# A graph network kernel: one tile of gathered rows in 25, 64 and 32 fetched row by row from SP and ScalarE, and features and output as 112 and 15 partitions

## The reference

```python
x = _layernorm(x + _L0_gnn_ref(x, edge_attr_64, edge_index, ...))   # sums of edge_attr_64 by src and by dst, then an MLP
x = _layernorm(x + _L1_gnn_ref(x, edge_attr_16, u, ...))            # mean of edge_attr_16 by dst, then an MLP
x = _layernorm(x + _L2_gnn_ref(x, weight, src, dst, edge_type_16))  # x[src] @ weight[type], summed by dst
x = _layernorm(x + _L3_gnn_ref(x, edge_index, edge_attr_32, ...))   # MLP on x[src], x[dst], edge; mean and max by dst; MLP
```

## Time and profile before

| | |
|---|---|
| median of 3 runs | 13071.3 us |
| the three runs | 13071.3, 13152.06, 13070.82 us |
| the profiled execution's own time | 13160.62 us, span 13158.9 us |
| busy share POOL, DVE, PE, ACT | 73%, 47%, 21%, 10% |
| mean granted clock of TensorE | 0.558 |
| first edge stage | about 280 to 4250 us |
| second edge stage | 4798 to 8718 us |
| third edge stage | 9035 to 12917 us |
| last node stage | 12928 to 13159 us |

### The profile page before, as it was taken

How to read it: one execution, slowest core, us unless ns; L and a number is a source line. 1 busy time by engine, 2 the same in 40 slices (tenths; PEclk the granted TensorE clock), 3 DMA queues, 4 the chain that set the end, 5 groups by cost and what they waited for, 6 DMA issues and landing times. The chain is left out here.

```text
span 13158.9 us, 78994 instructions
## 1 busy us (share of the span) xinstructions
PE 2819.3 (21%) x12129; PEld 1989.0 (15%) x12156; DVE 6175.8 (47%) x21573; ACT 1273.1 (10%) x3641; POOL 9662.0 (73%) x10101
## 2 busy tenths in 40 slices
PE   2000011111100740000000000013444444444446
PEld 2000011111100420000000000012232332332233
DVE  8877357777733432222222222224555555555554
ACT  3111011111110320000000000000000000001011
POOL 7777757777777747777777777777777777777774
PEclk6555555555555665555555555555666666666665
DMA  5444334444443332222222222222222222222221
GB/s 168 119 118 115 108 106 118 117 116 118 115 119 108 124 103 66 65 66 64 67 64 67 64 67 64 67 51 55 66 66 66 66 64 66 65 66 66 66 66 32
DMA packets 731549, 1103.24 MB, mean 84 GB/s; under 512 B 240731, under 2 KB 347192, under 8 KB 730567
## 3 DMA queue, kind: packets, MB, share of 16 engines
q0 software_dynamic: 332944, 306.83, 12.6%
q1 hardware_dynamic: 231478, 567.25, 11.4%
q10 hardware_dynamic: 167040, 228.30, 5.7%
HBM read 548.64 MB, written 552.93 MB: 84 GB/s over the span
## 5 line engine op out<-in xcount | busy, mean ns | idle before, releaser
L130 POOL DMA_INDIRECT msg<-Y,idx x3125 | 2965.9, 949 | 1060.1 <-issue 951.8
L130 POOL DMA_INDIRECT g<-in_edge_attr,idxs x3072 | 2948.7, 960 | 1017.7 <-issue 858.3
L130 POOL DMA_INDIRECT yg<-ytab,idx x3125 | 2951.8, 945 | 962.4 <-issue 950.0
L1520 DVE SCALAR_TENSOR_TENSOR run<-run,same,msg 128x64 f32<-128x64 f32 x3125 | 890.7, 285 | 3030.5 <-DMA msg<-Y,idx 2923.0
L584 DVE SCALAR_TENSOR_TENSOR run<-run,sameD 128x80 f32<-128x80 f32 x3072 | 906.3, 295 | 1396.9 <-DMA g<-in_edge_attr,idxs 875.2
L1914 DVE SCALAR_TENSOR_TENSOR run<-run,same,ps 128x32 f32<-128x32 f32 x3125 | 774.9, 248 | 1640.7 <-PE ps L1808 1538.0
L1108 PE MATMUL ps<-tail,before 128*128 128x64 f32 (+2 forms) x10 | 2.8, 422 | 4575.7 <-PEq L1422 3931.0
L1897 DVE SCALAR_TENSOR_TENSOR zx<-zx,same,zs 128x32 f32<-128x32 f32 x3124 | 792.1, 254 | 136.7 <-DVE anew L1880 29.1
L588 DVE SCALAR_TENSOR_TENSOR runS<-runS,sameS,g 128x64 f32<-128x64 f32 x3072 | 850.3, 277 | 0.0
L1789 PE MATMUL ps<-eaT,W1e 128*128 128x512 f32 (+1 forms) x394 | 401.6, 1123 | 1962.7 <-DMA yg<-ytab,idx 1962.1
L952 PE MATMUL ps<-hot 128*98 128x128 bf16 x3072 | 373.1, 315 | 1891.0 <-DVE hot L680 1891.0
(11 more groups left out here) (339 smaller groups left out, 6217.2 us busy)
## 6 DMA issues: line engine op xcount, KB each, us to landing
R<-run SPq DMA_DIRECT2D x390, 320.0 KB, 2.3
R<-run SPq DMA_DIRECT2D x195, 512.0 KB, 2.7
R<-run SPq DMA_DIRECT2D x124, 800.0 KB, 3.8
v<-in_edge_attr ACTq DMA_DIRECT2D x384, 256.0 KB
RA<-runS SPq DMA_DIRECT2D x256, 256.0 KB, 3.0
Y<-tab SPq DMA_DIRECT2D x98, 512.0 KB, 2.7
msg<-Y,idx POOLq DMA_INDIRECT x3125, 2.4
Z<-zeros SPq DMA_DIRECT2D x125, 400.0 KB, 4.3
```

The costliest lines, as they stand in the source:

```text
L130: eng.indirect_dma_start(out=out, out_offset=None, in_=table, in_offset=bass.IndirectOffsetOnAxis(ap=index, axis=0)).then_inc(sem, 16)
L1520: ins_ = v.scalar_tensor_tensor(out=run[:, q, t, :], in0=prev, scalar=same[:, q, t:t + 1], in1=msg[:, q, t, :], op0=ALU.mult, op1=ALU.add)
```

## The change

- In `edges_2` tile 12 of each slot's 25 is no longer gathered by POOL. Slots 0, 2 and 4 of a chunk leave it to SP, slots 1 and 3 to ACT: the engine loads 32 row offsets from a list into registers, issues 32 DMAs of one row each, and does that four times (`row_tile`, `fetch_rows`). Then it asks for the next chunk's list (`list_rows`). DVE waits for those rows by `by_row`.
- In `edges_3` the same for tile 8 of slot 1 of each of the 48 chunks, all by SP.
- In `edges_01` tile 7 of slot 3 in all chunks but 0 and CHB: partitions 0 to 63 by SP, 64 to 127 by ACT, in pieces of 24, 20 and 20 rows behind three of the four slots (`row_pieces`).
- The lists of byte offsets are computed by DVE (`list_tiles`, and two instructions in `chores`) and put to memory with partitions and columns exchanged: 128x32 and 128x64 elements for the first stage, 128x130 and 128x49 for the others. The last two puts stand on SP behind the load of x.
- x is loaded and the output stored as 112 + 15 partitions in place of 127; the one partition that is left (12,500 = 127 x 98 + 54) is as before.
- `nodes_3` keeps the 896 columns of a group as four stacks of 32 rows in 128 partitions by 256 columns. W4 is placed by zero columns around it (`W4z`), W5 is a block diagonal (`W5e`), W6 stands once per stack (`W6e`). The relus work on 128x256 in place of 32x512 and 32x384.

```diff
+MOSTP = LASTP // 16 * 16
+STACK = P // 32
...
+ROW_AT2, ROW_AT3, ROW_SLOT3 = 12, 8, 1
+ROW_REGS = 32
+ROW_Q1, ROW_AT1 = NQ - 1, SG - 1
+PIECES1 = ((0, 24), (24, 20), (44, 20))
+SP_ROWS = (0, 2, 4)
...
+def fetch_rows(nc, eng, offsets, out, table, size, sem):
+    n = out.shape[0]
+    for a in range(0, n, ROW_REGS):
+        _, rows = nc.values_load_multi_w_load_instructions(
+            offsets[0:1, a:min(a + ROW_REGS, n)], engines=[eng.engine], min_val=0, max_val=table.shape[1] - size,
+            skip_runtime_bounds_check_because="the byte at which a row of the table begins")
+        for i, row in enumerate(rows):
+            eng.dma_start(out[a + i:a + i + 1, :].bitcast(U8), table[:, bass.ds(row, size)]).then_inc(sem, 16)
 
...
+        def list_rows(eng, i, c):
+            eng.dma_start(lists1[:, i, :], k.rows1[bass.ds(c, 1), i * P // 2:(i + 1) * P // 2]).then_inc(listed[i], 16)
+        def row_piece(eng, i, c, j):
+            a, n = PIECES1[j]
+            if j == 0:
+                eng.wait_ge(listed[i], 16)
+                eng.sem_clear(listed[i])
+            fetch_rows(nc, eng, lists1[:, i, a:a + n], g64[i * P // 2 + a:i * P // 2 + a + n, ROW_Q1, ROW_AT1, :], e64_bytes,
+                       4 * D, by_row)
+            if j == len(PIECES1) - 1:
+                if isinstance(c, int) and c == CHB - 1:
+                    eng.wait_ge(rows1_put, 32)
+                    list_rows(eng, i, CHB + 1)
+                elif not (isinstance(c, int) and c == C2 - 1):
+                    list_rows(eng, i, c + 1)
+        def row_pieces(eng, i, c, q):
+            if q == NQ - 1:
+                if not (isinstance(c, int) and c + 1 in (CHB, C2)):
+                    row_piece(eng, i, c + 1, 0)
+            elif q < len(PIECES1) - 1 and by_rows(c):
+                row_piece(eng, i, c, q + 1)
 
...
+                if q == ROW_Q1 and by_rows(c):
+                    v.wait_ge(by_row, 16 * P)
+                    v.sem_clear(by_row)
                 v.wait_ge(metas, n + 1)
-                v.wait_ge(got[q], 16 * SG * (c + 1))
+                if q == ROW_Q1:
+                    v.wait_ge(got[q], 16 * gathered(c))
+                else:
+                    v.wait_ge(got[q], 16 * SG * (c + 1))
...
+            def chunk(c, out, c0):
                 for q in range(NQ):
-                    turn_over(c, q, RB, 0)
+                    turn_over(c, q, out, c0)
+                    row_pieces(sp, 0, c, q)
...
+            chunk(CHB - 1, RB, 0)
             sp.wait_ge(x_clear, 1)
-            sp.dma_start(k.X[0:LASTP, :, :], ins["x"][0:LASTP * NB, :].rearrange("(p b) f -> p b f", b=NB)).then_inc(settled, 16)
+            for a, z in ((0, MOSTP), (MOSTP, LASTP)):
+                sp.dma_start(k.X[a:z, :, :], ins["x"][a * NB:z * NB, :].rearrange("(p b) f -> p b f", b=NB)).then_inc(settled, 16)
             sp.dma_start(k.X[LASTP:LASTP + 1, 0:LASTN, :],
...
-                    turn_over(c, q, RA, CHB)
+            sp.wait_ge(rows_listed, 2)
+            for to, rows in ((k.rows2, rows2[:, :, :].rearrange("p c q -> p (c q)")), (k.rows3, rows3[:, :])):
+                sp.dma_start(to.rearrange("n p -> p n"), rows, allow_slow_non_contiguous=True).then_inc(settled, 16)
+            chunk(CHB, RA, CHB)
+            with sp.Fori(CHB + 1, CE) as c:
...
-                    for t in range(SG):
+                    for t in range(SG - (q == ROW_Q1 and by_rows(c))):
                         gather(pool, g64[:, q, t, :], ins["edge_attr_64"], idxs[:, q, t:t + 1], got[q])
...
                     iteration(c, q, idxA if last else idxB, sameA if late else sameB, CHB if last else 0, CHB if late else 0)
+                    row_pieces(act, 1, c, q)
...
+        def row_tile(eng, c, q):
+            eng.wait_ge(listed[q], 16)
+            eng.sem_clear(listed[q])
+            fetch_rows(nc, eng, lists[:, q, :], msg[:, q, ROW_AT2, :], Yb, 4 * D, by_row[q])
...
+            for q in SP_ROWS:
+                row_tile(sp, 0, q)
             with sp.Fori(0, LAST) as c:
                 for q in range(NS2):
                     slot(c, q)
+                    if q in SP_ROWS:
+                        row_tile(sp, c + 1, q)
             for q in range(NS2 - 1):
                 slot(LAST, q)
...
+                        row_tile(act, c, q)
+            for q in range(NS2):
...
                 for t in range(SL2):
+                    if t == ROW_AT2:
+                        continue
                     gather(pool, msg[:, q, t, :], k.Y, idx[:, q, t:t + 1],
                            late[t // PART2] if last_slot(c, q) else got[q])
 
...
                         if last_slot(c, q):
-                            v.wait_ge(late[t // part], 16 * part)
+                            v.wait_ge(late[t // part], 16 * (part - (t // part == ROW_AT2 // part)))
+                            if t // part == ROW_AT2 // part:
+                                v.wait_ge(by_row[q], 16 * P * CHUNKS2)
                         else:
-                            v.wait_ge(got[q], 16 * SL2 * (c + 1))
+                            v.wait_ge(got[q], 16 * (SL2 - 1) * (c + 1))
+                            v.wait_ge(by_row[q], 16 * P * (c + 1))
...
+            def row_tile(c):
+                sp.wait_ge(listed, 16)
+                sp.sem_clear(listed)
+                fetch_rows(nc, sp, lists[:, :], yg[:, ROW_SLOT3, ROW_AT3 * MSG:(ROW_AT3 + 1) * MSG], ytab, 4 * MSG, by_row)
+                list_rows(c + 1)
+            list_rows(0)
+            row_tile(0)
+            with sp.Fori(0, LAST) as c:
                 for q in range(NS3):
                     store(c, q)
+                    if q == ROW_SLOT3:
+                        row_tile(c + 1)
+            for q in range(NS3):
+                store(LAST, q)
+            sp.wait_ge(listed, 16)
...
                 for a, b, w in cuts(steps):
                     nc.tensor.matmul(ps(1, q)[0:w, a:b], k.W1e[0:w, 0:w], eaT[0:w, m, a:b], start=True, stop=False)
+                    if a == 0:
+                        if by_rows(c, q):
+                            pe.wait_ge(by_row, 16 * P)
+                            pe.sem_clear(by_row)
+                        pe.wait_ge(got[q], 16 * (SL3 - (q == ROW_SLOT3)) * c + 16 * (steps - by_rows(c, q)))
...
                 a, z = g0 * GB, g1 * GB
-                sp.dma_start(most[:, a:z, :], k.X[0:LASTP, a:z, :]).then_inc(saved, 16)
-                saves += 1
+                for i, j in ((0, MOSTP), (MOSTP, LASTP)):
+                    sp.dma_start(most[i:j, a:z, :], k.X[i:j, a:z, :]).then_inc(saved, 16)
+                    saves += 1
...
-                last.then_inc(outp, 1)
+                both = psY[q][:, 0:(GB - 1) * D].rearrange("p (j c f) -> p j c f", c=2, f=D)
+                nc.tensor.matmul(both[:, :, 1, :], h2[:, P:2 * P], k.W6e[:, 0:STACK - 1, :], start=False, stop=False)
+                nc.tensor.matmul(both[:, :, 0, :], h2[:, 0:P], k.W6e[:, 0:STACK - 1, :], start=False, stop=False)
+                nc.tensor.matmul(psY[q][:, (GB - 1) * D:], h2[:, 0:P], k.W6e[:, STACK - 1, :], start=False, stop=True)\
+                    .then_inc(outp, 1)
 
             def body(c, ahead):
...
+                            n = min(2, GB - 2 * j) * P
+                            last = nc.tensor.matmul(psH[:, 0:n], k.W4z[:, (STACK - 1 - j) * MSG:(2 * STACK - 1 - j) * MSG],
+                                                    catT[:, 2 * j * P:2 * j * P + n], start=j == 0, stop=j == 2)
+                    last.then_inc(hid, 1)
 
                     if later(c, q):
                         output(g - 1, 1 - q)
...
+                    nc.tensor.matmul(psH2, k.W5e[:, :], h1[:, :], start=True, stop=True).then_inc(hid2, 1)
 
```

148 lines of the change are left out of this document (105 added, 43 removed).

## The result

The changed kernel takes 13,340.8 us, median of 4 runs (13,333.8 to 13,355.9), beside 13,071.3 of the kernel before: ratio 1.0192, 95% interval 1.0152 to 1.0232. Forecast were 12,620 us, range 12,530 to 12,880. The profiled run has a span of 13,332.1.

What follows compares the result with a forecast made beforehand. POOL's gathers, back to back every 1.25 us, were taken to bound the edge stages. Terms -334 - 49 - 46 - 27 + 5 = -451 took the profiled 13160.6 to 12,710, less 89 to 12,620 us; range 12,530 to 12,880.

Steps and rivals of the forecast that it cites:

- Gathers at 1.25 us: Edge stages: POOL starts a gather every 1.25 us, so 267 removed gathers give -334 us (117, 156, 60 by stage).
- A row at 0.33 us: SP and ScalarE: each one-row DMA costs 0.33 us, taken from a bias load, between bounds of 0.27 and 0.47.
- the first rival: Second stage: a row costs SP over 0.338 us and SP becomes the bound; 12,720 to 14,270 us; no chance of its own.
- TENSOR_LOAD at 1.0 us: SP and ScalarE: loading up to 32 offsets into registers costs 1.0 us, 12 us a chunk on SP in the second stage.
- SP's 147 us: Second stage: SP's rows, loads, stores and lists sum to 147 us a chunk, against POOL's 150.
- the second rival: Second stage: register loads make SP the bound, from 1.25 us a load; 12,960 to 14,650 us; no chance of its own.
- its case of 2.4 us: Second stage: at 2.4 us a register load, SP needs 164 us a chunk, +340, giving 12,960 us.
- four signs named for this rival: Second stage: SP's rows back to back, DVE waiting for SP, POOL for ScalarE, gaps over 1.25 us ahead of each 32.
- First stage: First edge stage: SP's 29 and ScalarE's 34 us fit in 38.75 a chunk, so removed gathers give their full 117 us.
- x: First stage: loading x as 112 + 15 partitions gains 79 us, new list puts stall 30; the section's net is -49.
- Output and nodes_3: Kernel end: output as 112 + 15 partitions gives -46 us, stacked nodes_3 -27 us; together -73.
- The 89 us carried over from profile to median: Whole kernel: the median lies 89 us below the profiled execution, cause unknown; subtracted to turn 12,710 into 12,620.

Runs made afterwards that it cites:

- e6: Changed kernel with four row tiles per chunk in the second stage (SP 0 and 2, ScalarE 1 and 3), first-stage rows only behind the sort: 12,753.3 us, ratio 0.974.
- e13: Changed kernel, first-stage rows only behind the sort in two pieces, list puts in four parts, second-stage rows split evenly between SP and ScalarE: 12,653.8 us, ratio 0.968.
- e7: Changed kernel without first-stage rows (later stages' lists still put), SP's second-stage row tile between the slot's two stores: 13,278 and 13,380 us.
- e15: The kernel before, unchanged, profiled a second time: one run, 13,072 us.
- e12: The kernel before, unchanged, profiled on a slow chip: 15,699 us.
- e2: Changed kernel with ScalarE's two second-stage row tiles given back to GpSimd's gathers, SP keeping its three, on the slow chip: 20,428 us, ratio 1.294.
- e1: Changed kernel with no rows by SP and ScalarE in the second stage, on the slow chip: 17,537 us, ratio 1.111.
- e4: Changed kernel with one TENSOR_LOAD per second-stage row tile in place of four, on the slow chip: 20,144 us, ratio 1.276.
- e5: Changed kernel with no rows by SP and ScalarE in any stage and no puts of their lists: 12,901.7 us, ratio 0.984.

## Why the prediction was wrong, step by step

**Gathers at 1.25 us: right.** Third stage -61 against -60; with four and with five tiles by row (e6, e13) the second stage got 127 and 154 us shorter, against 125 and 156 by the count.

**A row at 0.33 us: right in size, and partly by luck.** It is 0.333 with gaps, below the break-even of 0.338, and the first rival did not come. But it isn't made as I had it: the DMA is issued in 0.228 us, the lower bound's 0.23, and a register move of 0.03 with its gap stands ahead of each, which no term had.

**TENSOR_LOAD at 1.0 us: this step failed.** I had bounds of 0 and 2.4 and a break-even of 1.25, and took 1.0 with no row behind the choice. Three of four take 2.12 us, the first of a tile 4.07 to 4.63 in the middle: 32 us a chunk instead of 12. With it the loop's end, about 2.5 us between its branch and the next instruction, which no term had. SP's 147 us became 174, above POOL's 150: the second rival, at a price above its case of 2.4 us since each tile's first load stands behind stores. The time came out 381 us above that rival's 12,960: 10 us more a chunk, and the 160 us of the first stage, whose full gain that rival kept. All four signs named for this rival came: SP's rows back to back, DVE waiting for SP's DMAs, POOL waiting for ScalarE's copies, and gaps of over 1.25 us ahead of each 32 rows.

The Trainium skill (Runtime: NRT & Kernel Launch, instruction fetch mechanics) says about 200 ns per register, told of loads from HBM. The loads here are from SBUF and don't follow it: 0.056 us a register with the fixed part taken off, 0.066 with it in, where that rule would make a load 6.4 us. The Trainium skill (DMA: Bandwidth & Descriptors, latency and other measured facts) gives a floor of about 600 ns for a tensor load. The changed kernel agrees with it, as its shortest of 1256 took 1.42 us, but a floor is no price for 32 registers.

**First stage: this step failed too.** I compared ScalarE's busy time with the chunk, 34 of 38.75 us, and found it to fit. But the pieces are part of a cycle that also holds the landing and the scan of slot 3; 34 + 2.4 + 3.4 is 39.8, which is what the trace of the changed kernel has from piece to piece. The landing and the scan were readable in the trace I had; the 34 held loads at 1.0 us, which measured 1.4 to 2.8, so that the sum meets the measured cycle to the tenth is luck. The check I made (the last piece has 15 us) took only one part of it. Of the 78 us behind the sort none came until a piece, with its load, was taken out. And "DVE's slack and the four gather buffers take up" the fetches behind pieces was wrong: +65 us in the sorting part against -39 counted.

**x: right.** 84 us gained without lists (79 counted), 23 lost by the puts (30 counted; SP held 45, 50 counted). The 50 was a choice between 12 and 162, so its nearness is luck. POOL's longest wait in the first stage was to fall to about 30 us and is 42.2, with rows in the stage; in e7, without them, it is 20.9.

**Output and nodes_3: right.** -79 against -73: the tail went from 51 to 3.5 us (-47, counted -46), the rest is the node stage (-32, counted -27). From one W5 product to the next it is 9.2 us (mean of 12 groups), as forecast, after 11.3 before.

**The 89 us carried over from profile to median: right,** and e15 shows where they are: in one node stage, at a granted clock of 0.67 instead of 0.85.

With the measured changes of the two failed stages put in for the forecast ones, 12,620 + 564 + 159 = 13,343, which is the time measured within 2 us; that the other errors cancel so nearly is luck. The range's lower end doesn't matter here, but it isn't what its words give: with the x and node terms in full (-79 and -46) the sum gives about 12,565, not 12,530.

## What to carry to other kernels

- A new instruction whose price the trace doesn't show, on the engine whose sum fits by 2%, is the forecast: with a break-even inside its bounds the chances should have been near even, and the value near the upper bound, since its nearest row was that one.
- Where a buffer is refilled only after its last use, add up the whole cycle (issue, landing, use), not the busy time of its engines. One piece less on the cycle gave 80 us; the change with its 94 gathers less had given that stage 7.
- Half a tile less on the engine that has no room, and pieces that leave the cycle slack, turned 1.9% slower into 3.2% faster than before. But that holds only where the kernel before takes 13,070 us: where it took 15,698, the same kernel was 25% slower than it.

## What the runs showed of the hardware that I had not expected

On the slow chips DVE and SP don't work slower, they start later. The kernel before in e12, DVE's timeline in the second stage, and for comparison the first profile, where three such scans take 0.93 us together:

```profile
7009.63 0.28 DVE L1520 SCALAR_TENSOR_TENSOR run<-run,same,msg 128x64 f32<-128x64 f32 x1 [1.11 <-issue]
7011.03 0.28 DVE L1520 SCALAR_TENSOR_TENSOR run<-run,same,msg 128x64 f32<-128x64 f32 x1 [1.11 <-DVE run L1520]
7012.43 0.28 DVE L1520 SCALAR_TENSOR_TENSOR run<-run,same,msg 128x64 f32<-128x64 f32 x1 [1.11 <-DVE run L1520]
```

```profile
6999.90 0.93 DVE L1520 SCALAR_TENSOR_TENSOR run<-run,same,msg 128x64 f32<-128x64 f32 x3
```

Each scan takes 0.28 us in both; the starts stand 1.40 us apart instead of 0.32. Over the second stage of e12 nearly all the steps from scan to scan are 0.7, 1.4, 2.1 or 2.8 us. In e2, about one in six of the steps from SP's register move to the DMA behind it, which waits for nothing, takes 0.7 or 1.4 us instead of 0.06. POOL is different: six in ten of its gathers there take the usual 0.94 to 0.95 us, but others take up to 1.94 where the longest before was 1.00, and the mean from start to start is 1.40 instead of 1.25. Both kinds of delay meet a kernel with 16,000 more DMAs of one row in one stage more often than one without; that this is all of the 25% isn't shown. Why a chip does this isn't settled; the chip numbered 9 ran e1 to e4 slowly and e13 to e15 at full pace.

A long loop on SP pays at its branch, in each pass (medians, branch to next instruction): 0.23 us with 37 instructions in the loop (second stage before) and 0.24 with 282 (third stage after), but 4.8 with 565 (e6) and 2.5 with 829 (second stage after). The page's DMA part (queue: packets, MB, share) has the instruction queue of the changed kernel and under it that of e5, which has no rows:

```profile
q14 instruction: 482, 3.95, 0.1%
```

```profile
q14 instruction: 71, 0.58, 0.0%
```

The changed kernel's trace has 372 of these packets in its second stage and 11 in its third, and one starts in each of the 23 gaps of the second. So the gap goes with instructions being fetched again; no run took the fetch away to prove it.
